# Setup order and step order of a cross-attention and expert network kernel on one core

## The reference, cut to what matters

```python
def xattn(x1, x2, memory_k, memory_v, Wq, bq, Wk, bk, Wv, bv, Wp, bp):     # 16 batches, 256 x 256, 16 heads of 16
    q = x1 @ Wq + bq
    k = concatenate([x2 @ Wk + bk, memory_k]);  v = concatenate([x2 @ Wv + bv, memory_v])
    attn = softmax(q k^T * 16 ** -0.5)             # per head, 256 x 512
    return (attn @ v) @ Wp + bp

def ffn(x, w_router, w_gating, w_gate, w_up, w_down):                      # 8 experts, 256 -> 1024 -> 256
    cw = softmax(x @ w_router) * softmax(x @ w_gating / 0.1);  cw = cw / (sum(cw) + 1e-9)
    h = silu(x @ w_gate[e]) * (x @ w_up[e])
    return sum over e of (h @ w_down[e]) * cw[e]

x = x + xattn(layernorm(x), fside, ctx, ctx, ...)
x = x + ffn(layernorm(x), ...)
```

## Time and profile before

| | |
|---|---|
| median of 3 runs | 2821.57 us (2820.4 to 2824.51) |
| the profiled execution | 2821.44 us |
| its span in the profile | 2819.1 us |
| PE / DVE / ACT / POOL busy | 2740.4 / 2202.1 / 1679.3 / 1719.8 us |
| granted TensorE clock, mean | 0.992 |

### The profile page before, as it was taken

How to read it: one execution, slowest core, us unless ns; L and a number is a source line. 1 busy time by engine, 2 the same in 40 slices (tenths; PEclk the granted TensorE clock), 3 DMA queues, 4 the chain that set the end, 5 groups by cost and what they waited for, 6 DMA issues and landing times.

```text
span 2819.1 us, 47288 instructions
## 1 busy us (share of the span) xinstructions
PE 2740.4 (97%) x16416; PEld 2235.2 (79%) x16416; DVE 2202.1 (78%) x3255; ACT 1679.3 (60%) x3238; POOL 1719.8 (61%) x1631
## 2 busy tenths in 40 slices
PE   6889999999999999999999999999999999999998
PEld 4668878787887878878788787878878788778887
DVE  7977788878788787877787888787887878776665
ACT  6756566565665666565665665656656565544443
POOL 5756566666666566656665665665665656654554
PEclk9999999999999999999999999999999999999999
DMA  2113223232332322333232322323323232233332
GB/s 68 35 57 96 77 91 99 90 101 73 97 97 87 105 78 91 94 94 95 83 97 80 106 89 79 102 78 106 94 76 102 74 100 90 91 105 109 105 105 82
DMA packets 251273, 252.25 MB, mean 89 GB/s; under 512 B 15904, under 2 KB 242848, under 8 KB 251040
## 3 DMA queue, kind: packets, MB, share of 16 engines
q1 hardware_dynamic: 251040, 249.25, 28.5%
HBM read 240.66 MB, written 8.52 MB: 88 GB/s over the span
## 4 chain that ended last, share of the span: by engine, by line
PE 82%; DVE 9%; issue 5%; ACT 4%; DMA 0%; POOL 0%; SPq 0%; ACTq 0%; POOLq 0%; DVEq 0%
PE ps_s L647 22%; PE ps_t L647 22%; PE ps_o L681 21%; PE ps_s L740 4%; PE ps_t L750 3%; PE ps_m L536 3%; DVE Pt_lo L1059 2%; PE ps_a L722 1%; DVE negmax L1120 1%; PE ps_a L724 1%; ACT h_hi L769 1%; PE ps_m L584 1%; DVE hf L926 1%; DVE X L1003 1%; DVE hf L919 1%
## 5 line engine op out<-in xcount | busy, mean ns | idle before, releaser
L931 DVE TENSOR_TENSOR h_lo<-hf,h_hi 128x512 fp32r<-128x512 f32 x512 | 557.9, 1090 | 355.2 <-ACT h_hi L769 350.6
L769 ACT ACTIVATE h_hi<-hf 128x512 fp32r<-128x512 f32 x512 | 323.7, 632 | 618.1 <-DVE hf L926 617.9
L1152 POOL TENSOR_TENSOR wg_lo<-stage_w,wg_hi 128x512 fp32r<-128x512 f32 x256 | 342.9, 1340 | 330.6 <-ACT wg_hi L776 327.9
L919 DVE SCALAR_TENSOR_TENSOR hf<-hf,ps_s 128x512 f32<-128x512 f32 x512 | 349.7, 683 | 199.0 <-ACT hf L764 190.9
L764 ACT ACTIVATE hf<-ps_s 128x512 f32<-128x512 f32 x512 | 306.3, 598 | 288.2 <-PE ps_s L647 171.5
L1212 POOL TENSOR_TENSOR Pt_lo<-Pt 128x512 f16<-128x512 f32 x256 | 288.5, 1127 | 251.6 <-ACT Pt L896 251.1
L681 PE MATMUL ps_o<-h_hi,wd_hi 128*128 128x512 f32 x1024 | 401.7, 392 | 1.2 <-DVE h_lo L931 1.2
L681 PE MATMUL ps_o<-h_lo,wd_hi 128*128 128x512 f32 x1024 | 400.4, 391 | 0.0
L681 PE MATMUL ps_o<-h_hi,wd_lo 128*128 128x512 f32 x1024 | 399.8, 390 | 0.0
L1152 POOL TENSOR_TENSOR wd_lo<-stage_w,wd_hi 128x512 fp32r<-128x512 f32 x256 | 341.0, 1332 | 90.7 <-ACT wd_hi L776 90.5
L926 DVE TENSOR_TENSOR hf<-hf,ps_t 128x512 f32<-128x512 f32 x512 | 347.4, 679 | 21.8 <-DVE hf L919 0.7
(11 more groups left out here) (190 smaller groups left out, 5081.5 us busy)
## 6 DMA issues: line engine op xcount, KB each, us to landing
stage_w<-in_L_ffn_w_gate_dram SPq DMA_DIRECT2D x256, 256.0 KB, 2.7
stage_w<-in_L_ffn_w_up_dram SPq DMA_DIRECT2D x256, 256.0 KB, 2.9
stage_w<-in_L_ffn_w_down_dram SPq DMA_DIRECT2D x256, 256.0 KB, 2.7
cwb<-d_cw SPq DMA_DIRECT2D x64, 256.0 KB, 3.5
X<-in_x_dram SPq DMA_DIRECT2D x32, 256.0 KB, 3.0
C<-in_fside_BxSxS_dram SPq DMA_DIRECT2D x16, 256.0 KB, 3.0
KVM<-in_ctx_dram SPq DMA_DIRECT2D x16, 256.0 KB, 2.6
d_x<-X SPq DMA_DIRECT2D x16, 256.0 KB, 2.1
```

What stands on the lines that cost most here:

```text
L769: act.activation(h_hi[f % FC][:], hf[:], ACT.Copy).then_inc(hh_done, 1)
L919: dve.scalar_tensor_tensor(out=hf[:], in0=hf[:], scalar=1.0, in1=ps_g[:], op0=ALU.add, op1=ALU.mult).then_inc(gate_done, 1)
L931: dve.tensor_tensor(h_lo[f % FC][:], hf[:], h_hi[f % FC][:].bitcast(F32), ALU.subtract).then_inc(hl_done, 1)
L1152: pool.tensor_tensor(lo[:], raw_weights(n), hi[:].bitcast(F32), ALU.subtract).then_inc(wl_done, 1)
```

## The change

Setup: bk and bv are loaded ahead of Wq, the memory context VF ahead of bq and bp, then Wp; each bias has its own semaphore. The identity copy and the clear of QTs are done by ScalarE ahead of its steps (QTs was GpSimd's, the identity VectorE's). The steps of turn -1: cT 1, xT 2, kv 4 and 6, q 9; high and low parts of Wk and Wv at step 2, of Wq at 3, of Wp and the router at 27 and 28; memory stack at step 5 instead of 2; bias scaling at 8 instead of 2. Values of batch 0: quarters 0 and 1 at steps 25 and 29 of turn -1 (instead of 15 and 21), quarter 2 at step 1 of turn 0 (instead of 29 of turn -1). Steps: hidden_of directly behind gate_of on VectorE, high_of directly behind weights_ahead on ScalarE.

```diff
-        w_in = [sem(f"w_in{n}") for n in range(5)]; b_in = sem("b_in"); b_scaled = sem("b_scaled")
+        w_in = [sem(f"w_in{n}") for n in range(5)]; b_in = [sem(f"b_in{m}") for m in range(4)]; b_scaled = sem("b_scaled")
-                self.qs_at, self.ks_at, self.ms_at = (10, 8, 2) if b == -1 else (18, 12, 13)
+                self.qs_at, self.ks_at, self.ms_at = (10, 8, 5) if b == -1 else (18, 12, 13)
-        FIRST_AT = {"cT": (1,), "kv": (3, 7), "xT": (5,), "q": (9,)}
+        FIRST_AT = {"cT": (1,), "xT": (2,), "kv": (4, 6), "q": (9,)}
-        HIGH_AT = {(-2, 9): (0, 1), (-1, 4): (2,), (-1, 16): (3, 4)}
-        LOW_AT = {(-2, 27): (0, 1), (-1, 4): (2,), (-1, 16): (3, 4)}
+        HIGH_AT = {(-1, 2): (0, 1), (-1, 3): (2,), (-1, 27): (3, 4)}
+        LOW_AT = {(-1, 2): (0, 1), (-1, 3): (2,), (-1, 28): (3, 4)}
+        FIRST_V = {-1: ((0, 25, 1), (1, 29, 1)), 0: ((2, 1, 0),) + V_AT}
+
+        def v_at(turn):
+
+            return FIRST_V[turn.b] if turn.b in FIRST_V else V_AT
...
+                def load_bias(m):
+                    eng.dma_start(bias[:, m], (bq, bk, bv, bp)[m].rearrange("(o n) -> o n", o=1).broadcast_to([P, D])).then_inc(b_in[m], 16)
+
                 for n, w in enumerate((Wk, Wv, Wq, Wp)):
+                    if n == 2:
+                        load_bias(1)
+                        load_bias(2)
                     if n == 3:
-                        for m, v in enumerate((bq, bk, bv, bp)):
-                            eng.dma_start(bias[:, m], v.rearrange("(o n) -> o n", o=1).broadcast_to([P, D])).then_inc(b_in, 16)
                         eng.dma_start(VF[:, QT:KC, :], one(c2_v, Turn(-1), 1)).then_inc(c2_in.sem, 16)
+                        load_bias(0)
+                        load_bias(3)
...
+            act.wait_ge(ident_done, 2)
+            act.activation(ident_r[:], ident[:], ACT.Copy).then_inc(ident_done, 1)
+            act.wait_ge(const_ready, 2)
+            act.activation(QTs[:].rearrange("p r h n -> p (r h n)"), zeros[:, 0, 0:1].broadcast_to([P, QRING * 2 * N]),
+                           ACT.Copy).then_inc(const_ready, 1)
...
                         weights_ahead(f)
+                        if f + 1 < FSTEPS:
+                            high_of(f + 1)
...
-                    for o, at, d in V_AT:
+                    for o, at, d in v_at(turn):
...
-                    if f is not None and f + 1 < FSTEPS:
-                        high_of(f + 1)
...
-            dve.wait_ge(ident_done, 2)
-            dve.tensor_copy(ident_r[:], ident[:]).then_inc(ident_done, 1)
...
                         gate_of(f + 1)
+                        hidden_of(f + 1)
                     for n in LOW_AT.get((turn.b, step), ()):
                         split_low(n)
-                    if turn.b == -1 and step == 2:
-                        dve.wait_ge(b_in, 16 * 4)
+                    if turn.b == -1 and step == 8:
+                        dve.wait_ge(b_in[0], 16)
...
-                    if f is not None and f + 1 < FSTEPS:
-                        hidden_of(f + 1)
...
+                            if turn.b == -1:
+                                dve.wait_ge(b_in[1], 16)
+                                dve.wait_ge(b_in[2], 16)
...
-            pool.memset(QTs[:].bitcast(F32), 0.0).then_inc(const_ready, 1)
...
-                        pool.wait_ge(b_in, 16 * 4)
+                        pool.wait_ge(b_in[3], 16)
```

## The result

| | before | after |
|---|---|---|
| median | 2820.99 us (6 runs, 2815.44 to 2824.51) | 2796.82 us (6 runs, 2796.29 to 2798.86) |
| span of the profiled execution | 2819.1 us | 2794.7 us |
| PE / DVE / ACT / POOL busy | 2740.4 / 2202.1 / 1679.3 / 1719.8 | 2726.0 / 2173.4 / 1694.6 / 1737.4 |

The ratio is 0.9916, 95% interval 0.9903 to 0.9929. The forecast was 2796. The total was met, but its terms were not, and that is what there is to learn here.

The account below looks back on a forecast made before the run. TensorE, busy 397.2 of 400 us in the joint part, was taken as the bound, so only its holes could be won back; 2821.4 less 22 (steps) and 4 (setup) gave 2795.4, told as 2796, range 2788 to 2811.

Parts of the forecast that it names:

- The sum: Whole kernel: 22 us gained in the steps and 4 in the setup, told as 2796 us.
- Setup: Before the network: first score 5.6 us earlier, less 1.0 and 0.6 for moved work; gain 4 us, bounds 1.5 and 5.3.
- the 1.0 said: Setup: splits, value copies and high parts moved to a busier place among the first maxima cost 1.0 us, bounds 0.3 to 1.7.
- The third quarter in turn 0: Its value copy pair at steps 1 and 3, on a ScalarE without idle time, costs 0 to 0.84 us, taken as 0.6.
- what is won here stays won: Setup: all that follows the first score and key product is a chain, so time won there is kept.
- What goes: Steps: up waits 18.0 us, maximum waits 4.4, restarts 2.6 and half-rate stretches after 2 us holes 5.1 vanish.
- The ceiling of 30.1: Steps: the most that can be won, 30.1 us, from waits, restarts and half-rate products together.
- What is late next: Steps: down waits for h_lo, 2.6 us, plus 3.0 in three held-up turns and 2.5 half-rate loss; residue 8.1 us.
- Rival 1: Steps: wait moves to down, GpSimd's splits blocking cprod then h_lo, 1.0 us per turn in 13 turns; 2807 us, chance 0.15.
- Rival 2: Steps: all comes back as other waits, so they give nothing and the setup 4; 2817.5 us, chance 0.11.
- rival 3: ScalarE: copies ahead of key copies and exponentials make exponentials late, 3.6 us uncovered in 13 turns; 2842 us, chance 0.08.
- Rival 4: Setup gives nothing or costs while the steps gain; 2801 us, sign a first key product later than 32; chance 0.05.

Follow-up runs that it names:

- experiment 9: Kernel after with the router's first four small VectorE operations moved to the end of step 18, the other three to the end of step 20; 2776.62 us.
- experiment 6: Kernel after with cprod and css made as one-operand sum reductions instead of two-operand products, which weights the experts otherwise; 2778.42 us.
- Experiments 3: Kernel after with high_of back behind the stacks on ScalarE, hidden_of staying early on VectorE; 2805.43 us.
- experiment 4: Kernel after with hidden_of back behind the small operations on VectorE, high_of staying ahead of the stacks on ScalarE; 2797.46 us.
- experiment 1: Kernel after with hidden_of and high_of both put back, so the changed setup with the step order of before; 2816.23 us.
- steps-only kernel: Kernel before with both step moves, hidden_of and high_of, and the setup left as before; 2802.81 us.

## Why the prediction was right, and where it was not

- **The sum** was 26 us and 24.2 were measured; 2796 against 2796.82. That it fits so well is luck: two large errors of the steps cancelled, as told below.
- **Setup, said 4:** 3.0 at the first tanh. The chain was right: first score said 20.1, was 20.28; KVM add said 14.4, ended 14.9; clear of QTs said 2.0, was 1.89; the query's low part said 18.35, was 18.75. The window from score to key grew from 7.92 to 8.76, 0.84 for the 1.0 said. The third quarter in turn 0, 0.6 said, fits as well: the lead falls from 4.4 to 3.7 over the first four exponentials, though no run isolates what takes it. What failed is the sentence that what is won here stays won: the lead was 4.4 still at the 47th exponential and 2.9 at the 49th, where TensorE ran at the lower clock in the trace after (0.57 over 4 us) and not in the one before. No term stood for that, and what decides the clock there is open.
- **What goes:** the waits of up did go, all 16, and so did the thirteen of the maximum and the half-rate stretches. Right. The ceiling of 30.1 was too low: from before to experiment 9, whose products hardly wait any more, the network's part is 43.1 us shorter. The price of a hole was set too low. After f = 408 holes with 3.2 us of listed waits (0.68 + 0.17, 0.34 + 0.80, 1.21) gave 6.1 us, and a turn with a 2 us hole gained some 2.6 more than one with a short hole. A listed wait counts from the modelled end of the product before, which overlaps the next by 0.16 (0.39 long, 0.23 apart), and the restart and the late products around it come on top. The holes of 0.93 were counted as ten in thirteen turns; in the trace they are nine in twelve.
- **What is late next, said 8.1:** the place (down for h_lo, steps 19 and 20) was right, the size wrong. I had h_lo end between 1041.6 and 1042.0 on a count of 2.0 us for the small operations, that is with cprod blocked once. In every turn after, css was blocked too, and at step 20 cw and the scaling. 18.0 us of listed waits instead of 8.1 of all losses. The kernel after is 21.95 us longer than experiment 9 in the network's part. Here the rule of the Trainium skill, page "SBUF — State Buffer", section "Who interferes with whom", which I had made a rival with a chance of 0.15, is what happened: experiment 6 took one operand away and the block went with it. The trace adds that such a meeting does not always cost VectorE: css took 0.15 in nine of twelve turns before. Rival 1's mechanism was the true one in all twelve turns, with one reading put right: GpSimd's operation beside cprod and css is the output addition, in the rows of before too (2.53 for two from 1039.42), and not a weight split. Its time, 2807, was wrong because the ceiling was too low as well. The two errors, some 13 us in the ceiling and some 14 in what is late next, had opposite signs.
- **The step that failed in reasoning:** I gave the gain to hidden_of, and ScalarE's move only 0.55 us in the working. Experiments 3 and 4 show the opposite: 0.6 for VectorE's move on top of ScalarE's, 8.6 the other way round (0.3 and 6.0 from first to last tanh). The 3.06 us stall stood in the earlier trace rows and was named as the cause of VectorE's lateness, but was priced only through its effect on tanh.
- **Rival 2** (all comes back) and **rival 3** (late exponentials): neither. No wait for an exponential over 0.2 us is in the trace after. **Rival 4:** first key product at 29.04, not later than 32.

## What to carry to other kernels

Price the block of a small operation at the length of the other engine's operation beside it (1.3 us here), not at what it took in most turns; where it is blocked in some turns, another order can make that all turns. When work is moved out of one gap, look for where the same queue idles: the router operations are 20 us cheaper at the ends of steps 18 and 20 than a few microseconds away from there. And an order that brings a product forward only trades waits if the same small operations still stand between it and the last thing that is read.

## What the runs showed that was not expected

- A VectorE operation on 2 elements per partition took 1.32 us when it had two operands in SBUF and GpSimd was at work, 0.16 as a reduction of one. With two operands, started within 0.02 us of GpSimd's addition, it took either 0.15 or 1.3, and nothing between.
- Each hole of 2.0 us in TensorE beside the network, three in the trace before, was followed by some 3 us at the lower clock (0.88 over 14 us); holes of up to 1.35 (experiment 4) were not. But one of the four holes of 2.0 in experiment 1 was not either (2241.34, clock 1.00), and ahead of the network a hole of 2.62 was followed by the lower clock in the trace after and not in the one before. So the length of the hole alone does not decide.
- The kernel before ran between 2814.87 and 2831.47 over all its runs. Timed side by side, it spread over 9.1 us and the kernel after over 2.6; experiment 9, without the holes, spread over 7.8 again (2772.99 to 2780.75). What makes the time steady is open.
- One execution of the steps-only kernel was 8 us faster than its others, at a lower mean granted clock (0.943). Four turns without the block account for 5.5 us; the record of the clock, 0.95 even where products follow each other at the usual pace, stays open.
